# Diagonal score banks of an attention kernel: the causal mask moves from a TensorE product to an add-and-maximum on VectorE

## The chip, the cores and the metric

The kernel runs on one core of a Trainium2 chip. The metric is the device time in microseconds. Three runs of the kernel before took 387.53, 389.51 and 386.03 us, median 387.53. The execution that the profiler recorded took 387.2 us; its span, from the first to the last instruction of the program, is 385.5 us.

## What is computed

The reference is one transformer block with adaptive layer norm on x of shape 2 x 1024 x 128: normalise, scale and shift by columns made from c, causal attention of 16 heads of 8 dimensions with rotary positions, a gated residual, a second normalisation, and a feed-forward part in which a router picks one of 8 experts for each row. What matters here are the scores:

```
scores = jnp.einsum('bhqd,bhkd->bhqk', q, k) * scale
causal_mask = jnp.triu(jnp.ones((Tx, Tx), dtype=bool), 1)
scores = jnp.where(causal_mask, -jnp.inf, scores)
attn = jax.nn.softmax(scores, axis=-1)
out = jnp.einsum('bhqk,bhkd->bhqd', attn, v)
```

## The kernel before

**Tiling.** The 1024 rows of each of the 2 batches are cut into two halves of 512, four units in all, in the order (batch 0, half 0), (0, 1), (1, 1), (1, 0). The 16 heads form four groups of four. A unit and a head group make a step, so there are 16 steps: 0 to 3 are half 0, 4 to 11 are half 1, 12 to 15 are half 0.

**Two passes over the scores.** Pass A (function `pass_a`) computes scores with the query rows on the partitions, only to find each row's maximum. Pass B (`pass_b`) computes them again transposed, with the negated maxima as extra rows of the product, so that ScalarE can take the exponential straight from PSUM into pt (line 627). On the diagonal GpSimd then sets what lies in the future to zero (line 523), and `times_v` multiplies by v (line 1020). The sum of the exponentials comes out of a column of ones beside v, and the division is done after that. Pass B has no mask product.

**Banks of pass A.** `bank_jobs_a` cuts a step's pass A into jobs that each fill one PSUM bank of 512 columns. For each of the four row tiles r of a half there is one "diag" job (four heads, 128 keys each, on the diagonal), "tri" jobs for the earlier keys of the same half (r x 128 columns per head), and in half 1 four "sq" jobs (one head and the 512 keys of half 0 each). That is 11 banks per step in half 0 and 27 in half 1, 304 in all, of which 64 are diag. For each job VectorE takes the maximum over the keys (line 818, `tensor_reduce` from PSUM into tmax); after the last one of a step it reduces tmax to negm (line 748), GpSimd splits negm into three bf16 parts (negp, lines 494 to 497), TensorE transposes them (line 901), ScalarE copies them to negt, and DMAs put them under the query rows in qst, where pass B of that step reads them.

**The mask.** maska is a 128 x 4 x 128 bf16 tile, zero where the key is allowed and -2^127 in the future. Before a diag bank's four score products, TensorE multiplies the identity by maska into the bank (line 978), and the score products (line 983) are added to it.

**What sets the order.** `plan` puts pass A and pass B on a common line of slots; in a slot each engine does its share of one pass A bank, then of one pass B bank, then of what else was placed there: the preparation of later units (layer norm, q, k, v with rotation and splitting), the output part of earlier units (POST), the row maxima ("max1", "max2") and the loads of stacked q and k. Pass B of a step starts at least 8 slots behind its last bank of pass A. Until pass B starts, every slot has a warm-up product (line 962) behind its bank. Every engine works its list in order.

**Banks and waits.** Seven PSUM banks are used in turn by all takers: TensorE may write a bank again only when the reader of its seventh-last use is done, which for pass A is the semaphore s_max, counted up by line 818. The eighth bank collects the product with v. VectorE in its turn waits for s_a, counted up by the last score product of a bank.

Of the kernel before, what the change touches and what calls it, by code (L numbers as in the profile page):

```python
# [22 lines left out]
ALU = mybir.AluOpType  # L23
ACT = mybir.ActivationFunctionType
AX = mybir.AxisListType
# [4 lines left out]
P = 128  # L30
# [7 lines left out]
HG = 4  # L38
NG = H // HG
PARTS = 3  # L40
ROWS = PARTS * PARTS * HD
# [6 lines left out]
LOW = -(2.0 ** 127)  # L48
# [135 lines left out]
def adaln_block(nc, x, ct, wmod, wqkv, wsw, bcol, bv, wo, bo, wr, wfc, wpj, rope, out):  # L184
    slots, a_at, b_at, v_at, stages, a_end = plan()
# [24 lines left out]
    with ExitStack() as ctx:  # L210
        def sb(name, shape, dt=F32):
            return ctx.enter_context(nc.sbuf_tensor(name, shape, dt))
# [4 lines left out]
        def sem(name):  # L217
            return ctx.enter_context(nc.semaphore(name))
# [15 lines left out]
        identb = sb("identb", [P, P], BF16)  # L234
        maska = sb("maska", [P, HG, P], BF16)
# [29 lines left out]
        kst = sb("kst", [ROWSM, 2, H, HALF], BF16)  # L265
        v_sb = sb("v_sb", [P, B * 2 * TU, VPAD])
        tmax = [sb(f"tmax{i}", [P, 2, 3, TU, HG]) for i in range(2)]
        negm = sb("negm", [P, 2, HG, TU])
        negr = sb("negr", [P, HG * TU])
        negp = sb("negp", [P, 2, PARTS, HG * TU], BF16)  # L270
# [26 lines left out]
        s_ident, s_mask, s_consts = sem("s_ident"), sem("s_mask"), sem("s_consts")  # L297
# [10 lines left out]
        s_a, s_max = sem("s_a"), sem("s_max")  # L308
# [16 lines left out]
        def bank_of(kind, which):  # L325

            return ps[:, use_no[(kind, which)] % NB, :]
# [6 lines left out]
        def wait_read(eng, name, u, k=0):  # L334

            _, i, use = side((name, u), k)
            eng.wait_ge(s_sfree[i], use + 1)
# [301 lines left out]
        def _(dve):  # L639
# [165 lines left out]
            for half in range(2):  # L805
                last = dve.memset(tmax[half][:, :, 1], LOW)
# [3 lines left out]
            for i in range(slots):  # L810
                if i in a_at:
                    s, (kind, r, h0, nh, nk) = a_at[i]
                    dve.wait_ge(s_a, i + 1)
                    src = bank_of("a", i)[:, 0:nh * nk].rearrange("p (h k) -> p h k", h=nh)
                    if s >= 2 and a_at[i - 1][0] != s:
                        dve.wait_ge(s_negm, s - 1)
                    dst = tmax[STEPS[s][1]][:, s % 2, ("diag", "tri", "sq").index(kind), r, h0:h0 + nh]
                    dve.tensor_reduce(dst, src, AX.X, ALU.max).then_inc(s_max, 1)  # L818
                for st in stages.get(i, []):
                    run(st)  # L820

# [2 lines left out]
        def _(pe):  # L824
# [15 lines left out]
            def take(kind, which):  # L840

                n = use_no[(kind, which)]
                bank_free(n)
                reached[0] = n + 1
                return ps[:, n % NB, :]

            def fill(st, k=0):

                _, i, use = side(st, k)
                ap = take("side", (st[0], st[1], k))  # L850
                if use:
                    pe.wait_ge(s_sfree[i], use)
                return ap, s_side[i]
# [111 lines left out]
            def stack_ready(s):  # L965
                b, half, g = STEPS[s]
                for hf in ((0, 1) if half or b else (0,)):
                    pe.wait_ge(s_stack[hf][g], 2 * PARTS * 16 * (b + 1))

            def pass_a(i):  # L970

                s, (kind, r, h0, nh, nk) = a_at[i]
                b, half, g = STEPS[s]
                if i == 0 or a_at[i - 1][0] != s:
                    stack_ready(s)
                dst = take("a", i)
                if kind == "diag":
                    pe.matmul(dst, identb[:, :], maska[:, :, :].rearrange("p h k -> p (h k)"), start=True, stop=False,  # L978
                              skip_group_check=True)
                for j in range(nh):  # L980
                    h = HG * g + h0 + j
                    k0, kh = (r * P, half) if kind == "diag" else (0, half) if kind == "tri" else (0, 0)
                    last = pe.matmul(dst[:, j * nk:(j + 1) * nk], qst[0:ROWS, half, h, r * P:r * P + P],  # L983
                                     kst[0:ROWS, kh, h, k0:k0 + nk], start=(kind != "diag"), stop=True,
                                     skip_group_check=True)
                last.then_inc(s_a, 1)

            def pass_b(i):

                s, gi, (kt, kh, c0, _), (h0, nh), _ = b_at[i]  # L990
                b, half, g = STEPS[s]
                n, w = bank_no[i], HALF - c0
                if n == 0:
                    pe.wait_ge(s_ones, 1)
                if gi == 0 and h0 == 0:
                    pe.wait_ge(s_mstack[s % 2], 48 * (s // 2 + 1))
                dst = take("b", i)
                for j in range(nh):
                    h = HG * g + h0 + j
                    last = pe.matmul(dst[:, j * w:(j + 1) * w], kst[:, kh, h, kt * P:kt * P + P],  # L1000
                                     qst[:, half, h, c0:HALF], start=True, stop=True)
                last.then_inc(s_b, 1)
# [27 lines left out]
            for i in range(slots):  # L1030
                if i in a_at:
                    pass_a(i)
                if i in b_at:
                    pass_b(i)
                if i < min(b_at):
                    keep_warm(1)
                if i in v_at:
                    times_v(*v_at[i])
                for st in pe_at.get(i, []):
                    run(st)  # L1040
                    if i > max(b_at) and st[0] in WARM_POST:
                        if st[0] == "n3" or st[1] == last_piece(len(UNITS) - 1):
                            keep_warm(WARM_POST[st[0]])
# [46 lines left out]
```

## Time and profile before

| | |
|---|---|
| median of three runs | 387.53 us |
| the profiled execution | 387.2 us, span 385.5 us |
| TensorE busy | 348.8 us, 90% |
| VectorE busy | 260.3 us, 68% |
| ScalarE busy | 214.7 us, 56% |
| GpSimd busy | 96.8 us, 25% |
| line 818, maxima of pass A (VectorE) | 304 instructions, 187.6 us busy |
| line 978, mask products (TensorE) | 64 instructions, 25.5 us busy |
| line 983, scores of pass A (TensorE) | 576 instructions, 114.4 us busy |
| line 1000, scores of pass B (TensorE) | 384 instructions, 113.6 us busy |

In the profile TensorE is PE (PEld its weight loads), VectorE is DVE, ScalarE is ACT, GpSimd is POOL. Busy times of TensorE and durations of single matmuls contain an overlap: a matmul is recorded from its start to its modelled end, and the next one starts before that. The same holds, less strongly, for VectorE. The distance from one start to the next shows what an instruction costs its engine when work is queued behind it. A share over the whole span is a mean over stretches with different limits.

### The profile page before, as it was taken

The page shows a single profiled execution, that of the slowest core. Times are in us where ns is not written, and L with a number is a line of the kernel's source. Part 1 is how long each engine was busy: PE and PEld are TensorE (multiplying, and loading weights), DVE is VectorE, ACT ScalarE, POOL GpSimd, SP SyncE. Part 2 cuts the span into 40 slices and gives each one's busy share as a digit, 9 for nine tenths or more (in the row PEclk, how much of TensorE's full clock was granted, in tenths as well). Part 3 has the DMA queues.
Part 4 walks back from the last instruction along what each step waited for, and adds up shares of the span by engine and source line. Part 5 has one row for each costly group of instructions (what it writes and reads, how often), then busy time and mean ns, then how long its engine had stood idle before and what let it go on. Part 6 is the DMA issues. An engine that isn't in the chain of part 4 may idle for free.

```text
span 385.5 us, 6882 instructions
## 1 busy us (share of the span) xinstructions
PE 348.8 (90%) x2348; PEld 164.8 (43%) x2348; DVE 260.3 (68%) x569; ACT 214.7 (56%) x415; POOL 96.8 (25%) x182
## 2 busy tenths in 40 slices
PE   6978897999598999999999989999999999989876
PEld 3434443443253333444444433444434444435544
DVE  4569863887968977678687675686887776322254
ACT  5251353664255565784576654854677666684343
POOL 5014354426400423500403011101114034221110
PEclk9999987999889999999999987999999999997999
DMA  6467130220320001230230500500000000000000
GB/s 223 145 200 169 57 105 1 65 63 3 101 71 0 1 3 68 83 86 0 63 90 7 120 0 1 126 0 29 1 2 3 2 4 2 3 1 2 29 0 27
DMA packets 12737, 18.86 MB, mean 49 GB/s; under 512 B 3616, under 2 KB 8608, under 8 KB 12704
## 3 DMA queue, kind: packets, MB, share of 16 engines
q1 hardware_dynamic: 12416, 18.04, 16.5%
q8 instruction: 19, 0.31, 0.3%
q10 hardware_dynamic: 288, 0.39, 0.3%
q14 instruction: 14, 0.11, 0.1%
HBM read 12.98 MB, written 5.24 MB: 47 GB/s over the span
## 4 chain that ended last, share of the span: by engine, by line
PE 68%; issue 6%; DVE 6%; POOL 4%; ACT 4%; DMA 2%; SPq 1%; ACTq 0%; DVEq 0%; POOLq 0%
PE ps_o L1020 17%; PE ps L983 14%; PE ps L1000 14%; PE ps L954 4%; PE ps L978 3%; PE ps L941 3%; PE ps L890 2%; DVE tmax L818 2%; PE ps L908 2%; DMA qst<-negt 2%; DVE rot L727 1%; PE ps L947 1%; PE ps L929 1%; SPq L423 1%; PE ps L881 1%
## 5 line engine op out<-in xcount | busy, mean ns | idle before, releaser
L818 DVE TENSOR_REDUCE tmax<-ps 128x1 f32<-128x512 f32 (+3 forms) x304 | 187.6, 656 | 69.4 <-PE ps L983 68.6
L627 ACT ACTIVATE pt<-ps 128x512 f32<-128x512 f32 (+1 forms) x304 | 162.1, 575 | 111.2 <-PE ps L1000 109.7
L1000 PE MATMUL ps<-qst,kst 75*128 75x512 bf16 (+3 forms) x384 | 113.6, 334 | 5.3 <-DMA qst<-negt 2.5
L983 PE MATMUL ps<-kst,qst 72*128 72x128 bf16 (+3 forms) x576 | 114.4, 279 | 1.0 <-DVE y L801 0.3
L1020 PE MATMUL ps_o<-pt,v_sb 128*32 128x512 f32 (+3 forms) x768 | 85.5, 518 | 5.6 <-POOL pt L523 5.3
L983 PEld LDWEIGHTS ps<-kst,qst 72*128 72x128 bf16 x576 | 49.8, 100 | 67.8 <-ACT pt L627 17.4
L523 POOL TENSOR_SCALAR_AFFINE_SELECT pt<-pt 128x512 f32<-128x512 f32 x64 | 40.2, 637 | 81.5 <-ACT pt L627 81.2
L1000 PEld LDWEIGHTS ps<-qst,kst 75*128 75x128 bf16 x384 | 35.5, 99 | 30.2 <-issue 6.0
L1020 PEld LDWEIGHTS ps_o<-pt,v_sb 128*32 128x32 f32 x768 | 15.7, 110 | 36.7 <-issue 21.4
L494 POOL CAST negp<-negm 128x16 bf16<-128x16 f32 x16 | 3.1, 196 | 100.4 <-DVE negm L748 100.2
L962 PE MATMUL ps<-maska,identb 128*128 128x512 bf16 x80 | 24.6, 422 | 3.3 <-POOL maska L460 3.3
L978 PE MATMUL ps<-maska,identb 128*128 128x512 bf16 x64 | 25.5, 398 | 0.8 <-DVE on L760 0.4
L478 POOL TENSOR_TENSOR rstd<-veps,mhalf 128x4 f32<-128x4 f32 (+1 forms) x9 | 8.5, 949 | 47.1 <-DVE veps L689 47.0
L794 DVE TENSOR_TENSOR fg<-ps,fg 128x512 f32<-128x512 f32 (+1 forms) x20 | 11.4, 578 | 10.4 <-PE ps L947 8.5
L954 PE MATMUL ps<-wpg,fg 128*128 128x128 f32 x128 | 17.2, 292 | 0.6 <-DVE fg L794 0.6
L954 PEld LDWEIGHTS ps<-wpg,fg 128*128 128x128 f32 x128 | 16.4, 205 | 2.9 <-ACT pt L627 1.6
L941 PE MATMUL ps<-h2t,wfc_sb 128*128 128x512 f32 (+1 forms) x40 | 17.4, 532 | 0.0
L570 ACT ACTIVATE part<-full 128x512 bf16<-128x512 f32 x8 | 5.0, 629 | 22.0 <-POOL full L360 16.8
L360 POOL TENSOR_TENSOR full<-rot 128x512 f32<-128x512 f32 x6 | 7.6, 1265 | 29.2 <-DVE rot L727 29.2
L727 DVE SCALAR_TENSOR_TENSOR rot<-ps,bcol_sb,rope_sb 128x512 f32<-128x512 f32 x16 | 11.3, 743 | 3.6 <-PE ps L890 3.6
L962 PEld LDWEIGHTS ps<-maska,identb 128*128 128x128 bf16 x80 | 8.4, 108 | 11.3 <-POOL maska L460 3.3
L589 ACT ACTIVATE ot<-ps_o 128x512 f32<-128x512 f32 x16 | 9.6, 599 | 5.8 <-PE ps_o L1020 5.8
(98 smaller groups left out, 267.2 us busy)
## 6 DMA issues: line engine op xcount, KB each, us to landing
qst<-qparts SPq DMA_DIRECT2D x48, 96.0 KB
kst<-kparts SPq DMA_DIRECT2D x48, 96.0 KB
qparts<-part SPq DMA_DIRECT2D x4, 384.0 KB, 2.6
kparts<-part SPq DMA_DIRECT2D x4, 384.0 KB, 3.5
xs<-in_x SPq DMA_DIRECT2D x4, 256.0 KB, 6.8
rope_sb<-in_rope SPq DMA_DIRECT2D x2, 512.0 KB, 5.9
qparts<-part SPq DMA_DIRECT2D x4, 256.0 KB, 2.9
qst<-negt SPq DMA_DIRECT2D x48, 4.0 KB, 1.7
```

The lines of the kernel that those rows point to most:

```text
L523: pool.affine_select(out=d, in_=d, compare_op=ALU.is_ge, fill=0.0, base=0, pattern=[[0, HG], [1, P]], channel_multiplier=-1).then_inc(s_tr ...
L627: act.activation(pt[:, G % NP, h0:h0 + nh, 0:w], src, ACT.Exp, scale=SCALE).then_inc(s_exp, 1)
L727: dve.scalar_tensor_tensor(out=rot[i][:, j], in0=src, scalar=bcol_sb[:, 2 * i + j:2 * i + j + 1], in1=rope_sb[:, j, HALF * u[1]:HALF * u[1 ...
L794: dve.tensor_tensor(fg[:, c, cols], src[:, cols], fg[:, c, cols], ALU.mult).then_inc(free, 1)
L818: dve.tensor_reduce(dst, src, AX.X, ALU.max).then_inc(s_max, 1)
L941: pe.matmul(dst[:, cols], wfc_sb[:, P * c:P * c + P], h2t[:, cols], start=True, stop=True).then_inc(full_, 1)
L954: last = pe.matmul(dst[:, D * t:D * t + D], fg[:, c, P * t:P * t + P], wpg[:, u[0], c], start=(c < c1), stop=(c == c1))
L962: pe.matmul(ps[:, reached[0] % NB, :], identb[:, :], maska[:, :, :].rearrange("p h k -> p (h k)"), start=True, stop=True)
L978: pe.matmul(dst, identb[:, :], maska[:, :, :].rearrange("p h k -> p (h k)"), start=True, stop=False, skip_group_check=True)
L983: last = pe.matmul(dst[:, j * nk:(j + 1) * nk], qst[0:ROWS, half, h, r * P:r * P + P], kst[0:ROWS, kh, h, k0:k0 + nk], start=(kind != "dia ...
L1000: last = pe.matmul(dst[:, j * w:(j + 1) * w], kst[:, kh, h, kt * P:kt * P + P], qst[:, half, h, c0:HALF], start=True, stop=True)
L1020: last = pe.matmul(ps_o[32 * j:32 * j + 32, 0, c0:HALF], v_sb[:, TU * (2 * b + kh) + kt, c:c + 32], pt[:, G % NP, j, 0:HALF - c0], start=( ...
```

## The change

In a diag bank TensorE no longer multiplies identity and mask; the four score products write the bank by themselves. VectorE reads the bank head by head: `tensor_tensor_reduce` adds the mask to the 128 scores of a row and takes the maximum, starting from -2^127. It writes the sums to a new SBUF tile, masked, which nobody reads, and the maximum to the same place in tmax as before. Every diag bank waits for the mask or for the end of the previous diag bank, which wrote masked too. The other 240 banks keep their maximum as it was. Old line 818 is line 829 now, and the new operation is line 825.

```
-                    dve.tensor_reduce(dst, src, AX.X, ALU.max).then_inc(s_max, 1)
+                    if kind == "diag":
+                        if i == 0:
+                            dve.wait_ge(s_mask, 1)
+                        else:
+                            dve.wait_ge(s_max, max(k for k in a_at if k < i and a_at[k][1][0] == "diag") + 1)
+                        for h in range(HG):
+                            last = dve.tensor_tensor_reduce(masked[:, h], src[:, h], maska[:, h], 1.0, LOW,
+                                                            ALU.add, ALU.max, dst[:, h:h + 1])
+                        last.then_inc(s_max, 1)
+                    else:
+                        dve.tensor_reduce(dst, src, AX.X, ALU.max).then_inc(s_max, 1)
...
                 dst = take("a", i)
-                if kind == "diag":
-                    pe.matmul(dst, identb[:, :], maska[:, :, :].rearrange("p h k -> p (h k)"), start=True, stop=False,
-                              skip_group_check=True)
                 for j in range(nh):
...
-                                     kst[0:ROWS, kh, h, k0:k0 + nk], start=(kind != "diag"), stop=True,
-                                     skip_group_check=True)
+                                     kst[0:ROWS, kh, h, k0:k0 + nk], start=True, stop=True)
```

VectorE, step 14, before (the first row ends step 13). Line 818 with 128x4 is four heads of 128 keys (diag, and tri for r = 1), 128x2 two heads of 256, 128x1 one head of 384 keys; line 748 ends a step.

```order
L748 TENSOR_REDUCE negm<-tmax 128x4x4
L818 TENSOR_REDUCE tmax<-ps 128x4 x4
L818 TENSOR_REDUCE tmax<-ps 128x2 x2
L818 TENSOR_REDUCE tmax<-ps 128x4
L818 TENSOR_REDUCE tmax<-ps 128x1 x4
```

The end of step 14 on VectorE in the changed kernel, its last diag bank and the tri banks around it. Line 825 is the new operation, which appears as instructions of a kind of its own (ISA).

```order
L829 TENSOR_REDUCE tmax<-ps 128x2 x2
L825 ISA masked,tmax<-ps,maska 128x128
L825 ISA tmax 128x1
L825 ISA masked,tmax<-ps,maska 128x128
L825 ISA tmax 128x1
L825 ISA masked,tmax<-ps,maska 128x128
L825 ISA tmax 128x1
L825 ISA masked,tmax<-ps,maska 128x128
L825 ISA tmax 128x1
L829 TENSOR_REDUCE tmax<-ps 128x1 x4
L749 TENSOR_REDUCE negm<-tmax 128x4x4
```

One maximum of 128x4 has become four pairs: one instruction over 128x128 and one that writes a 128x1 result. VectorE's list has 448 instructions more. On TensorE the rows of line 978, one in front of the four products of each diag bank, are gone, and nothing else has moved.

## Rows read from the trace of the kernel before

**Rows 1.** The page, part 1: busy us (share of the span) and instructions.
```profile
PE 348.8 (90%) x2348; PEld 164.8 (43%) x2348; DVE 260.3 (68%) x569; ACT 214.7 (56%) x415; POOL 96.8 (25%) x182
```

**Rows 2.** The page, part 4: the chain that ended last, by engine and by line.
```profile
PE 68%; issue 6%; DVE 6%; POOL 4%; ACT 4%; DMA 2%; SPq 1%; ACTq 0%; DVEq 0%; POOLq 0%
PE ps_o L1020 17%; PE ps L983 14%; PE ps L1000 14%; PE ps L954 4%; PE ps L978 3%; PE ps L941 3%; PE ps L890 2%; DVE tmax L818 2%; PE ps L908 2%; DMA qst<-negt 2%; DVE rot L727 1%; PE ps L947 1%; PE ps L929 1%; SPq L423 1%; PE ps L881 1%
```

**Rows 3.** Waits: who waited for whom, us in total, times, longest us.
```profile
DVE tmax L818 <- PE ps L983: 68.6, 93, 3.5
...
PEld ps L983 <- DVE tmax L818: 12.0, 19, 0.8
```

**Rows 4.** Busy times by stretch, us from the start; PEclk is the granted clock.
```profile
core 0: us, PE busy (x) PEld busy (x) DVE busy (x) ACT busy (x) POOL busy (x), PEclk, DMA share, GB/s
31.40:37.60 6.20, 5.55 (x44) 3.21 (x41) 6.17 (x13) 1.26 (x2) 3.57 (x3) 1.00 0.77 155
37.60:47.10 9.50, 7.71 (x43) 3.75 (x44) 7.80 (x16) 2.06 (x5) 3.10 (x6) 1.00 0.26 80
47.10:61.50 14.40, 10.65 (x85) 4.98 (x84) 7.50 (x18) 7.09 (x15) 9.44 (x20) 0.88 0.23 71
61.50:73.70 12.20, 12.20 (x86) 5.87 (x85) 8.16 (x18) 6.40 (x14) 2.50 (x5) 0.72 0.18 51
73.70:153.20 79.50, 70.26 (x460) 31.73 (x459) 65.08 (x145) 42.38 (x82) 26.12 (x38) 0.96 0.12 38
153.20:287.30 134.10, 129.42 (x874) 56.56 (x873) 98.55 (x186) 85.46 (x167) 21.32 (x46) 0.97 0.17 44
287.30:323.20 35.90, 35.18 (x298) 16.71 (x296) 27.64 (x51) 24.60 (x50) 10.15 (x26) 1.00 0.02 3
```

**Rows 5.** TensorE in order of time around one mask product: start, us, instruction.
```profile
205.42 0.39 PE L978 MATMUL ps<-maska,identb 128*128 128x512 bf16 x1
205.65 0.39 PE L983 MATMUL ps<-kst,qst 72*128 72x128 bf16 x4
205.87 0.38 PE L1000 MATMUL ps<-qst,kst 75*128 75x512 bf16 x1
```

**Rows 6.** VectorE in order of time, four places where instructions of one kind follow each other.
```profile
31.39 6.12 DVE L818 TENSOR_REDUCE tmax<-ps 128x4 f32<-128x512 f32 x11
...
54.70 0.88 DVE L737 TENSOR_TENSOR v_sb<-ps,bv_sb 128x128 f32<-128x128 f32 x4
...
114.60 0.37 DVE L687 BATCH_NORM_AGGREGATE mv<-stats 128x2 f32<-128x6 f32 x4
...
203.00 2.48 DVE L818 TENSOR_REDUCE tmax<-ps 128x1 f32<-128x512 f32 x4 [0.74 <-PE ps L983]
```

**Rows 7.** Groups of VectorE instructions by shape: busy us, mean ns, idle before, releaser.
```profile
L818 DVE TENSOR_REDUCE tmax<-ps 128x4 f32<-128x512 f32 x80 | 53.4, 685 | 18.1 <-PE ps L983 17.9
...
L737 DVE TENSOR_TENSOR v_sb<-ps,bv_sb 128x128 f32<-128x128 f32 x16 | 3.5, 280 | 0.0
...
L687 DVE BATCH_NORM_AGGREGATE mv<-stats 128x2 f32<-128x6 f32 x32 | 3.1, 156 | 0.1
...
L689 DVE TENSOR_SCALAR veps<-mv 128x2 f32<-128x2 f32 x2 | 0.3, 168 | 0.1
```

**Rows 8.** TensorE in order of time, two waits for GpSimd in brackets.
```profile
38.90 0.24 PE L901 MATMUL ps<-identb,negp 128*48 128x128 bf16 x1 [1.96 <-POOL negp L497]
...
60.44 0.43 PE L1020 MATMUL ps_o<-pt,v_sb 128*32 128x128 f32 x8 [3.07 <-POOL pt L523]
```

**Rows 9.** Waits from 287.3 to 323.2 us, steps 12 to 15.
```profile
DVE tmax L818 <- PE ps L983: 8.3, 16, 0.9
...
PEld ps L983 <- DVE tmax L818: 1.7, 2, 0.8
```

More of the change, by code:

```diff
@@ L267, in adaln_block @@
         tmax = [sb(f"tmax{i}", [P, 2, 3, TU, HG]) for i in range(2)]
+        masked = sb("masked", [P, HG, P])
         negm = sb("negm", [P, 2, HG, TU])
```

## The prediction

> **What bounds the kernel now.** The page comes first: TensorE is busy 90% of the span, VectorE 68%, ScalarE 56% [rows 1]. The chain of waits gives TensorE 68% and VectorE 6% of the span; the mask product (line 978) has 3.5% of it, and the maxima of pass A (line 818) 2.1% [rows 2]. So TensorE leads, and VectorE already appears on the chain. The waits say how close it is: VectorE sits idle for TensorE before 93 maxima, 68.6 us in all, while TensorE's weight loads for pass A wait 12.0 us, in 19 places, for a maximum that gives a bank back [rows 3]. A share over the whole span hides stages with different limits, so the last view is the busy time by stretch, cut where a step's first maximum starts [rows 4]. A step is one head group of one half of one batch; half 0 has 11 banks in pass A, half 1 has 27, and both have four diagonal banks. Seven stretches follow: step 0, step 1, step 2, step 3, steps 4 to 6, steps 7 to 11, steps 12 to 15. The reader is to see that VectorE has 6.17 of 6.2 us in step 0, that TensorE has 129.4 of 134.1 us in steps 7 to 11, and that in steps 12 to 15, the half-0 steps at the end, TensorE has 35.2 and VectorE 27.6 of 35.9 us.
>
> **What TensorE gives up.** 64 mask products go (16 steps, four banks each). The row says 398 ns for one, but matmuls overlap; by starts, the product at 205.42 us holds the place until 205.65 us [rows 5]. That is 0.22 us, and 64 x 0.22 = 14 us, which is also what the chain has (3.5% of 385.5 us = 13.5 us). Per step it is 0.88 us. The four 128-column products of a bank stay. So 14 us is the most that can be gained, and only where TensorE sets the pace.
>
> **What VectorE takes on.** One maximum of 128x512 becomes, for each of four heads, an add-and-maximum over 128x128 and, as the order of instructions shows, a second instruction that writes the 128x1 result: eight instructions in place of one. The old one: eleven banks in a row, seven of 512 columns and four of 384, took 6.12 us; four of 512 in a row took 2.48 us and one alone lasts 0.69, so a start-to-start of (2.48 - 0.69) / 3 = 0.60 us [rows 6, 7]. The trace has no such add-and-maximum. The nearest row for the main instruction is the sum for v, 128x128 out of PSUM with a second input from SBUF: four in 0.88 us, one alone 0.28 us, so 0.20 us each when they overlap [rows 6, 7]. For the write of one column the nearest rows are the aggregate of 128x2 (four in 0.37 us, 0.16 us alone, so 0.07 us each) and the small one of 128x2 at 168 ns, which nothing overlaps in its own duration [rows 6, 7]. Lower bound for a pair: 0.20 + 0.07 = 0.27 us. Upper bound: neither overlaps, because the second needs the end of the first: 0.28 + 0.17 = 0.45 us. I take 0.31 us, nearer the lower end, since every run of VectorE instructions in the trace overlaps its starts, with a little for the dependence. A bank then costs 4 x 0.31 = 1.24 us against 0.60: 0.64 us more, 2.56 us per step, 41 us in all. The bounds are 0.48 us (1.9 per step) and 1.2 us (4.8 per step). Unlike the 14 us, this comes on the engine that now has the idle time, so what counts is how much of that idle time a stretch has.
>
> A rule of the Trainium skill (Vector Engine (DVE) Microarchitecture Reference, Measured stream behaviour on trn2) puts a fixed cost of about 75 ns on every instruction beside its columns. The trace agrees: (0.60 - 0.20) us over 384 columns leaves 0.07 us fixed. By that rule a bank is about 4 x (208 + 76) ns = 1.14 us (an estimate), 0.54 us more, and the sum would be within 1 us of the third rival's below. Against the change as such speaks VectorE: DVE Perf Modes, section on the TRN2 errata: one large tile pays the fixed part once, many small ones pay it each.
>
> The wait added in front of a diagonal bank, for the previous diagonal bank's end, stands behind work of the same engine: between neighbours it costs the tail of one instruction, 0.28 - 0.20 = 0.08 us, at the one adjacent pair of a half-0 step: under 1 us in all. A maximum behind it starts that much later, and so does the bank that it frees.
>
> **Stretch by stretch**, on the profiled execution (387.2 us, span 385.5; the runs' median is 387.5, 0.3 above it, so the two are taken as one):
> - Steps 0 and 1. In step 0 VectorE runs eleven maxima without a gap, TensorE then stands 1.96 us for the row maxima that come out of them, and fills its slots with warm-up products [rows 6, 8]: all 2.56 us are added. In step 1 VectorE has 9.5 - 7.8 = 1.7 us idle: 2.56 - 1.7 = 0.9. Together +3.5.
> - Steps 2 and 3. VectorE is idle 6.9 and 4.0 us, which covers 2.56 each. TensorE loses 3.07 us to the GpSimd selection of pt [rows 8], which the mask product doesn't touch. Of 2 x 0.88 I count 1: -1.
> - Steps 4 to 6. VectorE has 65.1 of 79.5 us and gets 7.7 more, 72.8; TensorE has 70.3 and gives 2.6. VectorE would have 92% and carries the normalisation and the rotations too; here it becomes the busier one. The 2.6 are not gained, and bunches cost 1: +1.
> - Steps 7 to 11. VectorE 98.6 + 12.8 = 111.4 of 134.1 us; TensorE sets the pace and gives 4.4. A bank is taken again after seven uses, some three and a half pairs of a bank of pass A and one of pass B, about 3.5 us at 134.1 us over 5 x 27 pairs; a diagonal bank of 1.24 us fits in, unless it meets side work. I leave 1.4 for that: -3.
> - Steps 12 to 15. VectorE 27.6 + 10.2 = 37.9 us, against 35.9 now and 32.4 that TensorE would need. VectorE sets the pace: +2, and 1 for filling and draining: +3.
> - The tail behind 323 us has no bank of pass A: 0.
>
> Sum: 3.5 - 1 + 1 - 3 + 3 = +3.5, so 387.2 + 3.5 = 391 us. ScalarE, GpSimd and the queues get nothing new; the 14 us of TensorE are hidden, not lost: TensorE waits instead.
>
> **Rivals.**
> 1. Faster: the pair costs no more than its bound of 0.27 us. Then step 0 adds 1.9, step 1 0.2; steps 2 and 3 give 1.8, steps 4 to 6 2.6, steps 7 to 11 4.4, and steps 12 to 15 end at VectorE's 27.6 + 7.6 = 35.2, 0.7 less: 2.1 - 1.8 - 2.6 - 4.4 - 0.7 = -7.4, 380 us. For it speaks that every row of VectorE overlaps; against it that TensorE's 12.0 us of waits for maxima would have to stay as small with a busier VectorE.
> 2. Slower: the write of the column waits for its main instruction, and VectorE becomes the bound in all half-0 steps and beyond. The point from which it decides is where the extra fills VectorE's 8.3 us of idle time in steps 12 to 15: 0.52 us per bank, a pair of 0.28 us. At 0.45 us: +4.8 and +3.1 in steps 0 and 1, +0.8 in step 3, +5 in steps 4 to 6 (14.4 added to 14.4 idle), -1 in steps 7 to 11 (122.6 of 134.1), 27.6 + 19.2 - 35.9 = +11 in steps 12 to 15: +24, 411 us. Speaks for it: the two are dependent, and their kind isn't in the trace at all; against: no pair of rows in the trace runs one after the other without overlap unless it waits for a semaphore.
> 3. Near no change: the write costs only the tail of its main instruction, 0.08 us, a pair of 0.28 us, 0.52 us more per bank and 2.1 per step. Steps 0 and 1 +2.5, 2 and 3 -1.4, 4 to 6 0, 7 to 11 -3.6, 12 to 15 (36.0 us of VectorE, 0.5 for filling) +0.6: -1.9, 385 us.
> 4. TensorE's granted clock falls where it now waits. After the 3.07 us wait the stretch of step 3 shows 0.72 of full speed, between 1.2 and 2.4 GHz [rows 4, 8]; 12.2 us at 0.72 would be 8.8 at full speed, so one such place costs about 3 us. The waits that I forecast are under 1 us each, and it adds to rival 2 rather than stands alone.
> That the change does not do what it says can be left out: the mask products are gone from TensorE's order, and VectorE's has 512 new instructions in place of 64.
>
> **Chances and range.** My forecast 0.35, rival 3 0.22, rival 1 0.18, rival 2 with or without the clock 0.25. The bounds of the pair give 380 to 411; leaving out 2 in 10 at the ends, mostly above, the range is 379 to 406. The likeliest case alone, with a pair of 0.29 to 0.34, would be 387 to 397. A measurement tells about 1% from no change, 383.7 to 391.4 us: faster than that are rival 1 and the lower tail of rival 3, 0.22; within it the rest of rival 3 and half of my forecast, 0.35; slower the other half and rival 2, 0.43.
>
> **What the changed profile would show.** No rows of line 978; pairs on VectorE whose start-to-start, four to a bank, is 1.24 us; VectorE busy near 300 us; in steps 12 to 15 hardly any idle time of VectorE and TensorE's waits for tmax well over the 1.7 us of before [rows 9]; step 0 about 8.7 us long instead of 6.2; steps 7 to 11 about 3 us shorter. A bank of 1.1 us or less, or TensorE still busy over 97% in steps 12 to 15, would prove the forecast wrong towards faster; a bank over 1.5 us, towards slower.

## The result, and the profile after

The changed kernel takes 394.4 us (median of 4 runs, 391.49 to 394.96) against 388.1 us (median of 4, 386.03 to 389.51): 1.022 times the time of before, 95% interval 1.016 to 1.028. It is slower, as forecast, and near the 391 us of the forecast. The reason is another one. Ratios and intervals leave out runs more than 1.5% above the fastest of the same kernel (for e10, e13, e14 and e15 that leaves only 3 of the 19 runs of the kernel before, which lie at 380.1 to 384.5 us), while medians are given over all runs, so a ratio need not be that of the two medians.

The profiled execution has a span of 392.2 us, 6.7 more than before. The page of the changed kernel, part 1 and two groups of part 5 (columns as in [rows 1] and [rows 7]):

```profile
PE 352.4 (90%) x2284; PEld 165.3 (42%) x2284; DVE 275.6 (70%) x1017; ACT 213.9 (55%) x415; POOL 96.7 (25%) x182
...
L825 DVE CUSTOM_DVE_ANT_0 masked<-ps,maska 128x128 f32<-128x128 f32 x256 | 58.9, 286 | 12.2 <-PE ps L991 10.0
...
L825 DVE DVE_READ_ACCUMULATOR2_ANT tmax<- 128x1 f32 x256 | 21.2, 83 | 0.0
```

VectorE's busy time grew by 15.3 us, not by 41. TensorE's grew by 3.6 us, although 64 instructions went. The same stretches as in [rows 4], cut at the same banks, show where that comes from:

```profile
core 0: us, PE busy (x) PEld busy (x) DVE busy (x) ACT busy (x) POOL busy (x), PEclk, DMA share, GB/s
33.40:51.60 18.20, 13.84 (x76) 6.26 (x74) 16.05 (x83) 3.57 (x8) 6.82 (x9) 0.91 0.35 90
51.60:80.90 29.30, 25.34 (x158) 11.54 (x157) 17.76 (x91) 13.70 (x28) 12.34 (x26) 0.65 0.19 56
80.90:163.00 82.10, 72.13 (x450) 31.59 (x448) 68.64 (x229) 42.52 (x82) 25.58 (x36) 0.92 0.12 37
163.00:293.50 130.50, 125.53 (x853) 53.88 (x852) 102.76 (x326) 84.85 (x167) 21.05 (x46) 0.97 0.17 45
293.50:327.70 34.20, 32.68 (x283) 15.26 (x281) 30.89 (x163) 23.73 (x51) 10.30 (x27) 1.00 0.02 4
```

The rows are steps 0 and 1, 2 and 3, 4 to 6, 7 to 11, 12 to 15. PEclk is the mean granted clock of TensorE, as a share of full speed. Against before their lengths changed by +2.5, +2.7, +2.6, -3.6 and -1.7 us; what lies ahead of the first maximum by +2.0 (33.4 against 31.4) and the tail by +2.2 (64.5 against 62.3), together +6.7. Where the granted clock is as before, 0.97 and 1.00, the change gains. In steps 2 and 3 the clock is 0.65; before it was 0.88 and 0.72 in the two halves. Over the whole span the mean granted clock fell from 0.960 to 0.921. With the two levels of 1.2 and 2.4 GHz that is 2 x 0.040 x 385.5 = 31 us at the lower one before and 2 x 0.079 x 392.2 = 62 us after.

One stretch holds about half of the difference: 2 x 0.48 x 24 = 23 us at the lower level against 2 x 0.48 x 7 = 7 us before. The rest lies in shorter ones: the changed kernel has two more of them ahead of step 3 and one more in the tail. The changed kernel from 65 to 89 us, and before it the place where TensorE waits, with the same columns:

```profile
65.00:89.00 24.00, 24.00 (x136) 10.74 (x129) 14.72 (x69) 11.02 (x22) 6.05 (x13) 0.52 0.10 31
60.00:65.00 5.00, 2.04 (x21) 0.61 (x20) 2.13 (x5) 1.69 (x3) 4.85 (x10) 0.89 0.29 75
```

The kernel before at the same place, its low stretch and what follows:

```profile
62.00:69.00 7.00, 7.00 (x35) 3.42 (x33) 3.61 (x8) 2.38 (x6) 0.75 (x2) 0.52 0.01 2
69.00:86.00 17.00, 16.96 (x139) 7.74 (x136) 14.46 (x36) 11.90 (x24) 6.75 (x13) 1.00 0.25 72
```

Both kernels wait there for GpSimd, which makes the gated weights before its next pt (before: 3.07 us, [rows 8]; after: 2.96), and in both the clock falls about the end of this wait. Before, it is back after 7 us. After, it stays at the lower level for 24 us, in which TensorE is recorded as busy without a gap. The end of a matmul is modelled, so that does not say how much of the time its array worked. The order of time on TensorE in the changed kernel (columns as in [rows 8]) shows the wait and what half a clock does to the first products behind it:

```profile
61.27 0.38 PE L1007 MATMUL ps<-qst,kst 75*128 75x512 bf16 x1
64.61 0.66 PE L1027 MATMUL ps_o<-pt,v_sb 128*32 128x128 f32 x8 [2.96 <-POOL pt L524]
65.20 0.61 PE L991 MATMUL ps<-kst,qst 72*128 72x128 bf16 x4
65.60 0.63 PE L1007 MATMUL ps<-qst,kst 75*128 75x512 bf16 x1
```

The same product of 75x512 lasts 0.38 us ahead of the wait and 0.63 us behind it, and four score products hold their place for 0.40 us instead of 0.22 [rows 5].

VectorE's new pairs, at the start of step 12 in the changed kernel (start, us, instruction):

```profile
293.54 0.29 DVE L825 CUSTOM_DVE_ANT_0 masked<-ps,maska 128x128 f32<-128x128 f32 x1
293.75 0.08 DVE L825 DVE_READ_ACCUMULATOR2_ANT tmax<- 128x1 f32 x1
293.75 0.29 DVE L825 CUSTOM_DVE_ANT_0 masked<-ps,maska 128x128 f32<-128x128 f32 x1
...
294.39 0.08 DVE L825 DVE_READ_ACCUMULATOR2_ANT tmax<- 128x1 f32 x1
294.62 0.29 DVE L825 CUSTOM_DVE_ANT_0 masked<-ps,maska 128x128 f32<-128x128 f32 x1
```

The write of the maximum starts at the same time as the next head's main instruction. It adds nothing to the distance: from head to head it is 0.21 us, a bank 0.84 us. Only between adjacent diagonal banks, where the new wait stands, the next bank starts 0.23 us after the last write (294.62 behind 294.39) instead of with it: 0.23 us in each of the eight half-0 steps, under 2 us in all, where 0.08 each were forecast.

### The profile page after: what moved, and what is told of

Read it like the earlier page. It is cut to its first block, busy times and chain, and to the rows that moved or that the text cites. A ratio compares the mean times of both kernels' runs of the same rounds, so it can differ in the third digit from the quotient of the medians.

```text
span 392.2 us, 7252 instructions
## 1 busy us (share of the span) xinstructions
PE 352.4 (90%) x2284; PEld 165.3 (42%) x2284; DVE 275.6 (70%) x1017; ACT 213.9 (55%) x415; POOL 96.7 (25%) x182
## 4 chain that ended last, share of the span: by engine, by line
PE 62%; DVE 11%; issue 7%; POOL 4%; ACT 4%; DMA 1%; SPq 1%; ACTq 0%; DVEq 0%; POOLq 0%
PE ps_o L1027 16%; PE ps L991 13%; PE ps L1007 12%; DVE tmax L829 5%; PE ps L965 4%; PE ps L952 4%; PE ps L901 2%; PE ps L919 2%; PE ps L940 1%; DVE rot L728 1%; DVE masked L825 1%; ACT pt L628 1%; POOL pt L524 1%; DMA qst<-negt 1%; PE ps L958 1%
## 5 line engine op out<-in xcount | busy, mean ns | idle before, releaser
L829 DVE TENSOR_REDUCE tmax<-ps 128x1 f32<-128x512 f32 (+3 forms) x240 | 147.7, 649 | 44.4 <-PE ps L991 43.4
L1007 PE MATMUL ps<-qst,kst 75*128 75x512 bf16 (+3 forms) x384 | 117.0, 344 | 5.0 <-DVE rot L728 1.8
L991 PE MATMUL ps<-kst,qst 72*128 72x128 bf16 (+3 forms) x576 | 119.0, 289 | 2.0 <-DVE rot L728 0.6
L1027 PE MATMUL ps_o<-pt,v_sb 128*32 128x512 f32 (+3 forms) x768 | 87.2, 527 | 6.3 <-POOL pt L524 5.2
L991 PEld LDWEIGHTS ps<-kst,qst 72*128 72x128 bf16 x576 | 48.9, 103 | 78.7 <-issue 24.5
L825 DVE CUSTOM_DVE_ANT_0 masked<-ps,maska 128x128 f32<-128x128 f32 x256 | 58.9, 286 | 12.2 <-PE ps L991 10.0
L1007 PEld LDWEIGHTS ps<-qst,kst 75*128 75x128 bf16 x384 | 36.5, 102 | 31.3 <-issue 6.9
L973 PE MATMUL ps<-maska,identb 128*128 128x512 bf16 x80 | 25.7, 437 | 4.7 <-POOL maska L461 3.3
L825 DVE DVE_READ_ACCUMULATOR2_ANT tmax<- 128x1 f32 x256 | 21.2, 83 | 0.0
L952 PE MATMUL ps<-h2t,wfc_sb 128*128 128x512 f32 (+1 forms) x40 | 19.5, 598 | 0.0
L361 POOL TENSOR_TENSOR full<-rot 128x512 f32<-128x512 f32 x6 | 7.6, 1266 | 32.1 <-DVE rot L728 32.1
```

What stands on the lines that cost most here:

```text
L825: last = dve.tensor_tensor_reduce(masked[:, h], src[:, h], maska[:, h], 1.0, LOW, ALU.add, ALU.max, dst[:, h:h + 1])
L952: pe.matmul(dst[:, cols], wfc_sb[:, P * c:P * c + P], h2t[:, cols], start=True, stop=True).then_inc(full_, 1)
L973: pe.matmul(ps[:, reached[0] % NB, :], identb[:, :], maska[:, :, :].rearrange("p h k -> p (h k)"), start=True, stop=True)
L1027: last = pe.matmul(ps_o[32 * j:32 * j + 32, 0, c0:HALF], v_sb[:, TU * (2 * b + kh) + kt, c:c + 32], pt[:, G % NP, j, 0:HALF - c0], start=( ...
```

## The experiments

Two theories. **Theory 1, the clock**: TensorE is granted less clock because it has less work. **Theory 2, VectorE's work**: the 15 us more on VectorE hold TensorE up. The first four kernels take the two apart.

**e1: product kept as a filler, VectorE as in the changed kernel.**

```
 dst = take("a", i)
+if kind == "diag":
+    pe.matmul(dst, identb[:, :], maska[:, :, :].rearrange("p h k -> p (h k)"), start=True, stop=True)
```

> The changed kernel with the mask product kept on TensorE as a filler in all 64 diagonal banks (the score products then overwrite it); VectorE as in the changed kernel. TensorE has its old work, VectorE the new. Theory 1 (the change is slower because TensorE, with less to do, is granted a lower clock): the mean granted clock comes back from 0.92 to 0.95 or more and the stretch of 24 us at half clock behind 65 us is gone; 386 to 391 us. Theory 2 (it is slower because of VectorE's 15 us more): both engines are now loaded, 395 us or more whatever the clock.

Measured: 388.7 us over 10 runs, before 387.4 over 25 on the same chip; ratio 0.998, interval 0.991 to 1.006. Clock 0.955. VectorE's 15 us more are hidden, all of them within 1%; theory 2 falls. Behind the wait the clock is back after 10 us.

**e2: no mask on either engine.** The mask is left out of the row maxima of pass A; a maximum that is too large only shifts the exponent, and pass B removes the future by itself.

```
-if kind == "diag":
+if False:      # VectorE takes the old maximum in every bank
```

> The mask product is gone from TensorE and VectorE takes the single old maximum per diagonal bank: the mask is left out of the row maxima of pass A altogether, so a maximum may be that of a future key. Against before only TensorE's 14 us are taken away. Theory 1 (clock): granted clock 0.93 or less, and hardly a gain, 384 to 391 us. Theory 2 (VectorE's extra work ate the gain): the 14 us show where TensorE sets the pace, 374 to 382 us, clock as before.

Measured: 388.4 us over 10 runs, of which six lie between 384.1 and 389.2 and four at about 399 us with a clock of 0.893 to 0.901; ratio 1.002, interval 0.996 to 1.009; clock 0.933 in the profiled execution (384.6 us). TensorE's 14 us of work are gone, VectorE has nothing more than before, and nothing is gained that can be told. The time went to the clock: 2 x 0.067 x 382.9 = 51 us at the lower level, 20 of them in a row behind the wait, although VectorE has no added work here.

**e3: filler in steps 0 to 3 only** (`if kind == "diag" and s < NG`).

> The changed kernel with the filler product only in steps 0 to 3 (16 diagonal banks). Theory 1, with the cause in the early steps: the half-clock stretch from 65 to 89 us is gone as with the full filler, while steps 4 to 15 keep the product's time: 380 to 386 us, faster than before. Theory 2: 393 us or more, since VectorE is not relieved at all.

Measured: 383.7 us, ratio 0.984, interval 0.978 to 0.991; clock 0.964. Sixteen products that compute nothing turn 2% slower into 1.6% faster. The mean clock does not settle a time by itself: one of the ten runs took 383.3 us at 0.922.

**e4: steps 0 to 3 as before** (product with mask, one maximum), the rest as changed.

> Steps 0 to 3 as in the kernel before (mask product and one maximum), steps 4 to 15 as in the changed kernel. Theory 1: like the early filler, and some 2 us better, since steps 0 and 1 have no added VectorE time: 378 to 385 us. Theory 2: 12 of 16 steps keep VectorE's extra work, three quarters of the loss stays: 391 to 394 us.

Measured: 383.8 us over 4 runs, ratio 0.990, interval 0.976 to 1.004; clock 0.968. By the median it is e3 again, but the interval takes in no change; the 2 us expected beyond e3 are not seen.

The next four ask where the filler works, and what starts the fall.

**e8: filler in steps 0 and 1 only** (`s < 2`), and **e9: in steps 2 and 3 only** (`s in (2, 3)`), eight products each.

> The changed kernel with the filler only in the eight diagonal banks of steps 0 and 1, where warm-up products already stand in every slot. If it is TensorE's work ahead of the wait at 62 us that matters: as with the filler in steps 2 and 3, or less. If only the work around the wait counts: the half-clock stretch behind 65 us stays, 391 us or more.

Measured: 392.6 us, ratio 1.007, interval 1.001 to 1.014; clock 0.922, as in the changed kernel. The long stretch is still there. The ratio lies below the changed kernel's 1.022 and the intervals do not overlap, so a small part may have been won back; the two were measured on different occasions, and the medians are 1.8 us apart.

> The changed kernel with the filler only in the eight diagonal banks of steps 2 and 3, on both sides of the wait and in the half-clock stretch itself. If the work there ends the fall sooner: clock 0.95 or more and 381 to 386 us, as with steps 0 to 3. If the early steps decide: 390 us or more.

Measured: 383.0 us, ratio 0.985, interval 0.979 to 0.992; clock 0.947 in the profiled execution. Busy times of e9 behind its wait:

```profile
60.00:62.00 2.00, 1.26 (x12) 0.64 (x13) 0.00 (x0) 0.55 (x1) 1.37 (x6) 0.50 0.00 0
62.00:64.00 2.00, 2.00 (x13) 1.36 (x11) 1.26 (x11) 0.65 (x3) 0.51 (x1) 0.50 0.00 0
...
68.00:70.00 2.00, 2.00 (x14) 0.77 (x7) 0.48 (x1) 0.16 (x1) 0.00 (x0) 0.55 0.03 4
70.00:72.00 2.00, 2.00 (x23) 1.09 (x21) 2.00 (x11) 1.93 (x4) 0.98 (x2) 1.00 0.46 129
```

The clock still falls at the wait, but is back at 70 us, some 10 us later instead of 24. So the products of steps 2 and 3 count, and those of steps 0 and 1 do not shorten the stretch. Whether it is those of step 3, in the stretch itself, or also those of step 2, of which some stand ahead of the wait, was not taken apart.

The length of the low stretch behind this wait goes the same way in every profiled execution that has the wait. Where the product stands in steps 2 and 3 it is 7 us (before, e4, e15) or 10 us (e1, e3, e6, e9); where it does not, it is 24 us (the changed kernel, e8) or 20 us (e2). Most of this stretch in e8, and then in e2:

```profile
64.00:87.00 23.00, 23.00 (x115) 10.09 (x116) 14.02 (x67) 10.21 (x20) 5.42 (x12) 0.50 0.10 28
```

```profile
61.00:81.00 20.00, 20.00 (x97) 7.75 (x96) 11.13 (x29) 8.56 (x18) 5.02 (x10) 0.50 0.13 32
```

**e7: changed kernel, no filler, gated weights early.** GpSimd's six instructions (4 us) move from step 2 to the place before its work for step 0.

```
-    + [("gate", 0), ("q1", (0, 1))]
+    + [("gate", 0), ("gates", 0), ("q1", (0, 1))]
...
-    put(GATES_AT, "gates", 0)
```

> The changed kernel without any filler; GpSimd makes the gated weights (lines 503 to 505, 4 us) before its work for step 0 instead of in step 2. This takes away what TensorE waits 3 us for just before the half-clock stretch at 65 us. If that wait starts the long fall: no stretch of more than 7 us at half clock, mean clock 0.95 or more, 379 to 387 us. If the clock falls because TensorE has less work as such: the stretch stays or moves, clock 0.93 or less, 390 us or more.

Measured: 381.2 us, before 389.2; ratio 0.977, interval 0.972 to 0.982; clock 0.955. The wait is gone from TensorE's list. Busy times of e7 at steps 2 and 3, and the 10 us from 60 us on:

```profile
48.80:68.50 19.70, 18.53 (x159) 9.11 (x159) 17.29 (x92) 12.77 (x28) 7.68 (x17) 0.91 0.29 82
60.00:70.00 10.00, 9.83 (x88) 4.89 (x86) 9.79 (x54) 7.17 (x16) 4.11 (x12) 1.00 0.22 61
```

19.7 us for steps 2 and 3, against 29.3 changed and 26.6 before. Part of it is given back: steps 4 to 6 take 84.3 us (79.5 before). Two stretches of 10 us at the lower level stand there, from about 95 and from about 116 us (clock 0.52 from 96 to 106 and 0.50 from 116 to 126), where the expectation had none over 7. The span is 376.4 us. In steps 2 and 3 the product is missing as in the changed kernel, and from 60 to 70 us the clock stays up: at this place it is the wait that brings the fall, and the missing product that makes it long. Why falls at other places last 7 us in one kernel and 10 in another is left open.

**e6: no mask on either engine, filler in steps 0 to 3.**

> No mask in pass A's row maxima at all (left out on both engines), and the filler product in steps 0 to 3. Against the changed kernel with the same early filler (383.7 us) only VectorE's 15 us more are taken away. Clock theory with VectorE's work hidden: 381 to 385 us, no clear difference. If VectorE's extra work does cost where TensorE has less to do: 374 to 380 us.

Measured: 381.8 us, ratio 0.981, interval 0.976 to 0.987, next to e3's 0.984. Where the clock is looked after, VectorE's 15 us still cost nothing that can be told.

The last four ask what is left of the change once this fall is away, and from where VectorE's work would count.

**e10: kernel before with the gated weights early.**

> The kernel before, with GpSimd's gated weights made early as in the run that took the changed kernel to 381 us. It says what the change is worth when the 3 us wait in front of the half-clock stretch is gone from both. If the change is worth TensorE's 14 us less what stays hidden: 385 to 388 us here, 4 to 7 us above the changed kernel's 381. If the change is worth nothing without the clock, and the early weights bring it all: 379 to 383 us.

Measured: 385.2 us (10 runs), before 389.0 (19 runs); ratio 0.996, interval 0.983 to 1.009. The intervals of e10 and of e7 (0.977) against before just fail to overlap, and the medians are 4 us apart, so the change is probably worth about 1% there. The two were measured on different chips, and the single times of e10 reach from 378.7 to 390.3 us, so this stays likely, not shown. e14 below, ten runs on the same chip and occasion as e10, points the same way. In the profile of e10 steps 2 and 3 take 20.3 us, but steps 0 and 1 take 19.6 against 15.7 before, with a clock of 0.83: the early weights take part of their gain back there.

**e13: no mask on either engine, gated weights early.**

> No mask in pass A's row maxima at all (left out on both engines), gated weights early, no filler. The clock theory says that without the long fall the missing product and the missing VectorE work both count: 376 to 381 us. If it is above 384 us with a clock under 0.94, another long fall has taken the place of the first.

Measured: 377.5 us (4 runs), ratio 0.986, interval 0.960 to 1.012; clock 0.959. It has the lowest median of all, but the interval is too wide for a ranking.

**e14: changed kernel with filler in steps 2 and 3 and gated weights early.**

> The changed kernel with both remedies, the filler in steps 2 and 3 and the gated weights early. If both only remove the same half-clock stretch, they don't add up: 380 to 384 us, not better than the early weights alone. If the filler also helps elsewhere: 375 to 379 us.

Measured: 381.0 us (10 runs), ratio 0.987, interval 0.971 to 1.003. By the medians the two remedies don't add up (e7 alone 381.2), as both act on the same stretch. Against e10 the median is 4.3 us lower, and in 78 of the 100 pairs of one run each e14 is the faster, but the single times overlap widely.

**e15: e1 with one more maximum over each diagonal bank on VectorE.**

```
+dve.tensor_reduce(dump[:, :], src, AX.X, ALU.max)
 for h in range(HG):
     last = dve.tensor_tensor_reduce(masked[:, h], src[:, h], maska[:, h], 1.0, LOW, ...
```

> The filler in all 64 diagonal banks, as in the first experiment, and in front of VectorE's four pairs one more maximum over the bank, 0.60 us, whose result nobody uses. A diagonal bank then costs VectorE 1.44 us instead of 0.84, 38 us more in all; the forecast had assumed 1.24. If the sum of the forecast was right in all but the price of the pair: 393 to 402 us. If VectorE's work is hidden further than I reckoned: 386 to 391 us.

Measured: 411.7 us, ratio 1.076, interval 1.060 to 1.092, against 388.7 of e1: 38 us more on VectorE cost 23 us. That is above both expected ranges (393 to 402 us the higher), so the forecast's sum with only the price corrected charges too little for a busy VectorE; part of the difference may be the clock, 0.942 against 0.955 in the profiled executions. Steps 7 to 11 and 12 to 15 of e15, and then steps 12 to 15 of e1:

```profile
166.20:303.00 136.80, 127.47 (x864) 55.12 (x874) 113.45 (x347) 86.05 (x167) 21.34 (x46) 0.99 0.18 43
303.00:344.40 41.40, 36.86 (x294) 16.26 (x296) 39.75 (x179) 25.38 (x50) 10.20 (x26) 1.00 0.01 3
```

```profile
285.80:321.80 36.00, 34.87 (x294) 16.73 (x296) 31.35 (x164) 24.65 (x51) 10.21 (x26) 1.00 0.02 3
```

In steps 12 to 15 VectorE is busy 39.8 of 41.4 us: it sets the pace. At 0.84 us per bank, in e1, it has 31.4 of 36.0, and the stretch is as long as before. Between 0.84 and 1.44 us per bank lies the point from which VectorE decides, as the forecast had it (1.12). In steps 7 to 11 VectorE has 83% and the stretch is still 4.5 us longer than in e1 (132.3 us), with the clock at 0.99 in both: there VectorE's work costs before the sum of a stretch says so. That it comes in bunches would explain it, but was not tested.

## Why the prediction was right, and where it was not

The direction and the size were right, the sum was not: its terms missed in both directions, and that the total came out 3 us from the measured one was luck. By its own signs the forecast's mechanism was wrong: it named a bank of 1.1 us or less as proof against it, and a bank costs 0.84 us; VectorE is busy 275.6 us, not near 300, and step 0 lasts 7.5 us, not 8.7.

- **What TensorE gives up**: 14 us at most, 0.22 us each. Right where nothing else moves: steps 7 to 11 gave 3.6 us (forecast 3), steps 12 to 15 1.7.
- **The price of a pair**: the mis-sized term. Forecast 0.31 us, bounds 0.27 to 0.45, measured 0.21, below the lower bound. The bound counted an issue slot for the write of the column, and it takes none. A bank costs 0.24 us more than before, 15.4 us in all (VectorE's busy time: +15.3), not 0.64 and 41.
- **Steps 0 and 1**: forecast +3.5, +2.5 in the profile, with 0.24 us of extra work per bank instead of 0.64 and a clock of 0.91 beside it. e3 and e2 have +1.5 and +2.2, so not even e2, without any work added on VectorE, keeps the 15.7 us.
- **Steps 2 and 3**: forecast -1, measured +2.7. VectorE had the idle time as reckoned; the clock took it.
- **Steps 4 to 6**: forecast +1 for a busier VectorE, measured +2.6; with the filler in steps 0 to 3 it is +0.5. The low stretch reaches 7 us into steps 4 to 6.
- **Steps 12 to 15**: forecast +3, measured -1.7. The arithmetic was good and the price wrong: 27.6 + 16 x 0.24 = 31.4 us, measured 30.9, so TensorE kept the pace. With a bank of 1.44 us the same sum gives 27.6 + 16 x 0.84 = 41.0, and e15 measured 41.4.
- **The tail**: forecast 0, measured +2.2. No bank of pass A lies there. The clock does: from 375 to 380 us it stands at 0.50, where before it was 1.00. It is so in e1 too (tail 64.3 us), but not in e3 (60.8), with the same instructions. Whether such a fall comes in the tail is left open.
- **The start**: +2.0 us ahead of the first maximum. Kernels with the same instructions up to there begin between 30.2 us (e1) and 32.1 us (e3), so it need not be the change's. Only the changed kernel has a lower clock from 25 to 30 us, 0.66, where before, e1 and e3 have 1.00; why is left open.

The step that failed is the fourth rival. It named the mechanism and the place, the fall of the clock behind the 3 us wait in step 3, and then set it aside because the waits to be added were short. No wait had to be added. It was enough to take work away around the low stretch that was there already, at 0.72 in [rows 4]: it grew from 7 to 24 us. A product of 0.22 us, four in each step, looked like pure cost, and was part of what brought the clock back (e9 against the changed kernel).

How much the clock is worth can be read from the kernel before alone, of which 51 single runs on three occasions have their clock beside them. The four at 0.964 took 384.2 to 384.5 us, the 23 at 0.947 took 388.0 to 391.0, median 389.6: some 5.2 us over 0.017, or 3 us for each 0.01. If the slope holds further down, where no run of it lies, the kernel before would take 389.6 + 2.8 x 3 = 398 us at 0.919, where the changed kernel's runs lie (0.912 to 0.926), and that one takes 394.4. So at a like clock the change gains some 3 to 4 us, and the lower clock costs some 10; both are estimates, and e3's run at 0.922 shows how loosely a time can follow the mean clock. e1 against the changed kernel, two programs that differ in the product alone, gives 388.7 against 394.4 us directly.

The rule of the Trainium skill on a fixed cost per instruction (Vector Engine (DVE) Microarchitecture Reference, Measured stream behaviour on trn2) holds for the main instruction, 0.21 us for 128 columns, and not for the read of the accumulator, which costs nothing here. The warning of the Trainium skill against small tiles (VectorE: DVE Perf Modes, on the TRN2 errata) is given for sources in SBUF. Here, with scores from PSUM and the mask from SBUF, it holds in direction: four instructions of 128 columns take 0.84 us, one of 512 takes 0.60.

TensorE: Matmul & The Clock Gate of the Trainium skill says that the clock is throttled by default and that activity releases it (What's actually happening). The traces agree on the fall: about the end of an idle wait of 3 us it comes. On the release the run decides: TensorE is recorded as busy for 24 us in a row at the lower level, so being recorded as busy was not enough here.

## What to carry to other kernels

Before taking work off TensorE, look at the granted clock by stretch: where it stands at the lower level, products that seem idle may be what ends that stretch, and removing the wait in front of it did at least as well as keeping a filler (e7 0.977, e9 0.985, with intervals that overlap). Split a sum by stretches and test each term on its own: here a term nearly three times too large and a term left out gave nearly the right total. An engine with a third of its time idle hid 15 us of new work, and not 38 more.

## What the runs showed of the hardware

- The read of VectorE's accumulator (128x1, 83 ns in its row) starts together with the next instruction and adds nothing to the distance between heads, 0.21 us.
- TensorE can be recorded as busy for 24 us in a row and stay at 1.2 GHz (clock 0.52 from 65 to 89 us). With eight more products of 128x512 in steps 2 and 3 (e9) that time was 10 us, and without the 3 us wait ahead (e7) there was none at that place.
- The same kernel's time goes with the clock it happens to be granted: 380.1 to 392.6 us for the kernel before, at a mean clock of 0.973 down to 0.943.
